# Position products and the self-attention projection put in front of the transposes of the probabilities, and the copies of these transposes put in rising order

## The reference

```python
x = x + attn(layernorm(x))        # 16 heads of 8 channels; attn itself adds its input: h + out
x = x + xattn(layernorm(x), ctx)  # 16 heads of 64, rotary q and k, window j <= i and j >= i-32
x = x + ffn(layernorm(x))         # 8 experts, the best one per token, and a shared expert (SiLU)

# self-attention
qkv = h @ w_in.T + b_in;  attn = softmax(q k^T / sqrt(8)) v;  out = ctx @ w_out.T + b_out
# cross-attention
q, k, v = h @ wq.T, ctx @ wk.T, ctx @ wv.T          # 1024 wide
probs = softmax(rope(q) rope(k)^T / 8, masked);  out = (probs v) @ wo.T
# experts
idx = argmax(h @ router.T);  y = down[idx](silu(gate[idx] h) * (up[idx] h)) + the shared expert
```

## Time and profile before

| | us |
|---|---|
| median of 3 runs | 748.58 |
| lowest and highest of them | 747.98, 751.69 |
| the profiled execution | 752.78 |
| its span | 750.7 |
| TensorE busy in it | 714.9 (95%) |
| ScalarE busy | 533.8 (71%) |
| VectorE busy | 541.2 (72%) |
| GpSimd busy | 531.3 (71%) |

### The profile page before, as it was taken

The page is one execution under the profiler, slowest core; times in us unless marked ns, Lnnn a source line. Parts: engine busy times, 40 slices in busy tenths (PEclk is TensorE's granted clock), DMA queues, the critical chain, the costliest instruction groups (busy, mean ns, idle before and its releaser), DMA issues. The chain is left out here.

```text
span 750.7 us, 31278 instructions
## 1 busy us (share of the span) xinstructions
PE 714.9 (95%) x11673; PEld 593.3 (79%) x11673; DVE 541.2 (72%) x1406; ACT 533.8 (71%) x1943; POOL 531.3 (71%) x875
## 2 busy tenths in 40 slices
PE   6889999999999999999999999999999999789994
PEld 4667888888888888888888888888888888666563
DVE  2466777777777777788877877877877776646763
ACT  2267777877778888877777778777777777554452
POOL 3266677777778887777777777777777777736565
PEclk9999999999999999999999999999999999999998
DMA  6000000211111000000000000000000000142240
GB/s 240 4 18 9 7 9 14 73 38 38 38 38 38 17 17 26 24 25 24 25 24 24 25 24 25 25 25 20 20 16 30 10 10 10 35 130 69 78 124 20
DMA packets 22802, 27.61 MB, mean 37 GB/s; under 512 B 3448, under 2 KB 18684, under 8 KB 22656
## 3 DMA queue, kind: packets, MB, share of 16 engines
q1 hardware_dynamic: 19152, 17.80, 7.9%
q0 software_dynamic: 2784, 6.56, 2.4%
q10 hardware_dynamic: 720, 1.26, 0.5%
HBM read 16.82 MB, written 9.24 MB: 35 GB/s over the span
## 5 line engine op out<-in xcount | busy, mean ns | idle before, releaser
L1123 ACT ACTIVATE PX<-P,mx 128x128 f32<-128x128 f32 x512 | 186.7, 416 | 11.1 <-DVE mx L704 10.9
L1406 POOL TENSOR_TENSOR PX<-PX,mx 128x512 f32<-128x512 f32 x128 | 130.8, 1042 | 13.3 <-DVE mx L709 13.1
L1123 ACT ACTIVATION_READ_ACCUMULATOR PX<-P,mx 128x1 f32 x512 | 131.2, 256 | 0.0
L643 DVE TENSOR_REDUCE nmf<-P 128x4 f32<-128x512 f32 x128 | 79.5, 684 | 17.6 <-PE P L226 17.6
L704 DVE TENSOR_REDUCE mx<-P 128x4 f32<-128x512 f32 x128 | 83.0, 670 | 3.6 <-PE P L326 3.6
L1132 ACT ACTIVATE PT<-P 128x512 f32<-128x512 f32 x128 | 69.8, 599 | 20.2 <-PE P L339 20.2
L1401 POOL TENSOR_TENSOR rq<-rq,tq 128x1024 f32<-128x1024 f32 x32 | 75.9, 2371 | 2.9 <-DVE tq L668 2.9
L1396 POOL TENSOR_TENSOR rk<-rk,tk 128x1024 f32<-128x1024 f32 x32 | 76.0, 2374 | 0.0
L1366 POOL CAST nm<-nmf 128x16 bf16<-128x16 f32 x32 | 6.4, 201 | 97.0 <-DVE nmf L643 97.0
L291 PE MATMUL P<-wvT,cxT 128*128 128x512 f32 x128 | 70.9, 636 | 0.6 <-ACT nmT L1080 0.4
L1087 ACT ACTIVATE PS<-P 128x512 f32<-128x512 f32 x128 | 66.6, 614 | 3.7 <-PE P L247 3.7
(11 more groups left out here) (179 smaller groups left out, 1832.9 us busy)
## 6 DMA issues: line engine op xcount, KB each, us to landing
ew<-in_ew SPq DMA_DIRECT2D x9, 384.0 KB, 3.8
xrow<-z_xs SPq DMA_DIRECT2D x24, 136.0 KB
z_xs<-c SPq DMA_DIRECT2D x16, 136.0 KB, 2.9
x<-in_x SPq DMA_DIRECT2D x32, 64.0 KB, 2.1
cxT<-in_ctxT SPq DMA_DIRECT2D x31, 64.0 KB, 1.8
wk<-z_xs SPq DMA_DIRECT2D x6, 136.0 KB
wvT<-z_xs SPq DMA_DIRECT2D x6, 136.0 KB
tab<-in_tab SPq DMA_DIRECT2D x1, 512.0 KB, 8.7
```

The source lines that it names most:

```text
L643: dve.tensor_reduce(nmf[b % 2][:, 0, r, :], v3(bank(f"s{r}")), AX.X, ALU.max, negate=True).then_inc(S["v_bm"][r], 1)
L1123: t = act.activation(PX[(4 * b + r) % 6][:, c, :], p[:, c * 128:c * 128 + 128], ACT.Exp, bias=m[:, 0, r, c:c + 1], scale=1.0, accum_out=m[ ...
L1406: pool.tensor_tensor(X[:, :, :], X[:, :, :], mx[b % 3][:, 2, r, :].rearrange("p (h a) -> p h a", a=1).to_broadcast([128, 4, 128]), ALU.mul ...
```

## The change

Two pieces of the loop are reordered, one on TensorE and one on ScalarE. Prologue, tables and all functions stay as they are, and so do the lists of VectorE, GpSimd and the DMA queue. On TensorE `f_pos` and `a_qkv` now stand in front of the two `d_t` calls, and these are called in the order k = 0, 1. On ScalarE `a_q` stands in front of the four `d_pt` calls, and these are called in the order 0, 1, 2, 3.

```diff
@@ block.tensor, the loop over s
                 batch(r_q, s - 4, 1)
                 tile(x_tr, "xt", s - 36, 3)
                 tile(x_hT, "xr", s - 37, 3)
-                batch(d_t, s - 5, 1)
-                batch(d_t, s - 5, 0)
                 batch(f_pos, s - 8)
                 batch(a_qkv, s - 2)
+                batch(d_t, s - 5, 0)
+                batch(d_t, s - 5, 1)
                 batch(b_pv, s - 3)
@@ block.scalar, the loop over s
                 batch(b_ps, s - 3, 2)
-                batch(d_pt, s - 5, 3)
                 tile(x_hT, "xr", s - 37, 3)
+                batch(a_q, s - 2)
+                batch(d_pt, s - 5, 0)
                 batch(d_pt, s - 5, 1)
-                batch(d_pt, s - 5, 0)
-                batch(a_q, s - 2)
                 tile(x_xT, "xt", s - 36, 3)
                 batch(d_pt, s - 5, 2)
+                batch(d_pt, s - 5, 3)
                 tile(x_th, "xg", s - 36, 1)
                 batch(b_oT, s - 3)
```

## The result

The changed kernel takes 763.28 us (median of 4 runs, 761.96 to 765.27); the kernel before took 749.51 in the 4 runs beside it. The ratio is 1.0189 with a 95% interval from 1.0166 to 1.0213. On the earlier median of 748.58 this is 14.1 us more (12.4 to 15.9), where 11.0 had been forecast. The direction held, and 763.28 lies inside the stated range of 754.5 to 763.5, but at its upper edge and above the forecast's own range of 756.5 to 762.8.

The account below looks back on a forecast made before the run. The prediction took TensorE, busy for 95% of the span, as the bound. Its terms, 6.9 + 4.4 - 0.3 = 11.0 us on the median of 748.6, gave 759.6 us, with a stated range of 754.5 to 763.5.

Parts of the forecast that it names:

- TensorE is the bound, and a wait in its list shows in full: Whole kernel: TensorE, busy for 95% of the span, is never kept waiting; added waits show in the span nearly in full.
- Part 1: TensorE, loop: position products, moved ahead of the turns, wait for the last self-attention exponential (bank 4); 0.24 a period, 6.9 us.
- The chain hangs on `b_s`: Loop: maxima, exponentials and `b_ps` follow TensorE's own `b_s`, so the 0.24 lag is paid again in each period.
- The saved shape change: TensorE, before `b_pv`: one array shape change fewer would save 0.09 a period, 2.4 us, but lies inside the wait.
- Part 2: TensorE, loop: the second `d_pv` waits for the turned tiles' last copy; 0.17 a period, 4.4 us, as a new L353 row.
- Part 3: What comes earlier: mostly worth nothing, but in the last turns the first copy comes sooner, a gain of 0.3 us.
- The sum: Whole kernel: 6.9 + 4.4 - 0.3 = 11.0 us slower, 759.6 on the median; chance 0.64.
- No second wait: Rival, loop: ScalarE starts the turned tiles' copies sooner, so TensorE needn't wait for them; 755.2 us, chance 0.2.
- worked off: Rival, loop: ScalarE keeps its own beat and its exponentials catch up after a few periods; 748 to 750, chance 0.06.
- no wait at all: Rival, loop: position products don't wait and the saved shape change counts; 745.2 to 746 us, chance 0.05.

Follow-up runs that it names:

- e3: Changed kernel, but ScalarE's loop exponentials of self-attention read bank 4 first instead of last; ratio 1.0049 to the kernel before.
- e9: Changed kernel, but VectorE instead of ScalarE makes the fourth copy of turned tiles (r = 3); ratio 1.0129 to the kernel before.
- e10: Changed kernel with the edits of e3 and e9 together; ratio 1.0005 to the kernel before.
- e5: Kernel before, with two empty ScalarE instructions put in front of the self-attention exponentials; ratio 1.0000 to the kernel before.
- e6: Changed kernel, with two empty ScalarE instructions put in front of the self-attention exponentials; ratio 1.0228 to the kernel before.
- e4: Changed kernel, but position products put behind the turns again, query, key and value projection left in front; ratio 1.0016 to the kernel before.
- e2: Kernel before's order up to s = 34, the new order on both engines from s = 35 on; ratio 1.0026 to the kernel before.

## Why the prediction was right or wrong

- **TensorE is the bound, and a wait in its list shows in full.** Right. The loop grew by 11.40 us, and taking the waits away gave 8.7 (e3), 3.8 (e9) and 12.6 (e10) back.
- **Part 1, the wait for bank 4.** Right in place, count and size. 27 waits, 0.06 of latency behind the exponential's end, the second period's larger one too (20.78 there against 20.01). e3 takes 0.35 off the period: the 0.24 plus the 0.09 of the shape change, which it uncovers.
- **The chain hangs on `b_s`.** Right; e5 and e6 show it by adding to ScalarE's work.
- **The saved shape change.** Right as a gain that the wait swallowed. Once no wait is left, the period is 19.40 (e10), 0.10 below before, and 0.095 of it is found at the boundaries between the steps. e4's 0.10 is another gain, which no forecast had.
- **Part 2, the copies.** Right in place and size: 0.16 a period against 0.17, and e9 gives 0.16 back. Its announced sign was wrong: no row has L353 waiting for `PT` 26 times. The stall is inside the busy time, and was found by the distance between starts.
- **Part 3, the end.** This is the step that failed. It counted 0.3 us as gain ("It is now first, worth up to one pitch twice"), and e2 measured a loss of 2.0 (0.2 to 3.7). Half of its mechanism was there: in the last turns but one `d_pv` waits 0.8 for the copy instead of 1.2 (the rows of L353 above). But soon after it TensorE waits for a DMA in either order (L419), so it isn't shown that anything of this gain is left. The other half, the very last turns, went the other way. The step looked at the copies and named GpSimd's last normalization only in passing, without a price. In the last periods GpSimd is not ahead of TensorE any more, and the order k = 1, 0 had let half the turns run before the normalization r = 0 was there. With k = 0 in front, everything waits 2.03 for it, where 0.80 and 0.63 were waited before.
- **The sum.** 6.9 + 4.4 = 11.3 for the loop stands against 11.40. With the end's 2.0 in the place of -0.3 it would have been 13.3, a ratio of 1.0178, inside the interval. So the term that was off is the end. Only 0.6 of it is seen in the rows. Together with the loop's 11.40 that makes 12.0, and the other 2 us of the measured 14.1 have no place of their own. The measured difference is uncertain by 1.8 either way, so how much of them is real stays open.
- **The rivals.** "No second wait" is ruled out by e9, "worked off" by e6, "no wait at all" by the 27 waits.

## What to carry to other kernels

An instruction list that never waits may still be full of waits that its order hides. Before moving a step forward, read which semaphore it waits for, through the bank it reuses as well, and how long before its start the release came: here it was 0.95 us, and the step was moved by 1.14. Then treat the loop's last rounds on their own, since the engines' leads over each other are not the same there.

## What the runs showed that was not expected

- A stall shorter than a product's modelled duration raises TensorE's busy time instead of its idle time: L353 went from 50.0 to 54.6 us busy with the same count and a mean of 248 ns instead of 246, and back to 50.5 with a mean of 248 when the stall was removed (e9).
- The start behind a narrow product comes early mostly because the product is narrow, not because the shape change is cheap. `b_pv` starts 0.10 behind an 8-column product and 0.21 behind a 128-column one; the pitch of such products without a change is 0.03 and 0.11 to 0.12, so the change itself adds about 0.07 and 0.09.
- Most of the kernel's run to run scatter lies outside the loop. In the fourteen traces the first `b_pv` of the loop comes between 113.45 and 118.98 us, though the prologue is the same in all, while the loops of before, e2 and e5, which have one order and no wait, take 507.27, 507.08 and 506.97.
